# Three of four transposes per block move from TensorE to VectorE's 32x32 transpose (mLSTM block with a gated MLP)

## The reference

```python
xn = layernorm(x)
# mLSTM: 8 heads, 32 query/key and 64 value features each
q, k, v, o = xn @ Wq.T, xn @ Wk.T, xn @ Wv.T, xn @ Wog.T
i, f = soft_cap(xn @ Wig.T + big), soft_cap(xn @ Wfg.T + bfg)
h = mlstm_scan(q, k, v, i, f)                    # state carried over the tokens
att = (sigmoid(o) * multihead_norm(h, gamma)) @ Wout.T
# MLP, hidden size 2048
ffn = (silu(xn @ w_gate.T) * (xn @ w_up.T)) @ w_down.T
out = x + att + ffn
```

## Time and profile before

| | |
|---|---|
| Time, median of 3 runs | 3275.84 us (3273.61 to 3276.95) |
| The profiled execution's own time | 3273.61 us |
| Its span, first to last instruction | 3271.9 us |
| PE busy | 3101.0 us, 95% |
| DVE busy | 1876.5 us, 57% |
| ACT busy | 1116.8 us, 34% |
| POOL busy | 768.3 us, 23% |
| Granted TensorE clock, mean | 0.992 of full speed |

### The profile page before, as it was taken

How to read it: one execution, slowest core, us unless ns; L and a number is a source line. 1 busy time by engine, 2 the same in 40 slices (tenths; PEclk the granted TensorE clock), 3 DMA queues, 4 the chain that set the end, 5 groups by cost and what they waited for, 6 DMA issues and landing times.

```text
span 3271.9 us, 61574 instructions
## 1 busy us (share of the span) xinstructions
PE 3101.0 (95%) x22408; PEld 2229.5 (68%) x22408; DVE 1876.5 (57%) x4361; ACT 1116.8 (34%) x2142; POOL 768.3 (23%) x1126
## 2 busy tenths in 40 slices
PE   1499999999999999999999999999999999999999
PEld 0377777677776677776677776677776677776676
DVE  5565555565555565555665555655555655555654
ACT  3433333333333333333333333333333333333332
POOL 4322222222222222222222222222222222222122
PEclk9799999999999999999999999999999999999999
DMA  5000000000000000000000000000000000000000
GB/s 213 7 14 7 6 13 13 13 13 6 6 13 13 13 13 6 6 13 13 13 13 6 6 13 13 13 13 6 6 13 13 13 13 6 6 13 13 13 13 6
DMA packets 20333, 51.08 MB, mean 16 GB/s; under 512 B 1506, under 2 KB 1634, under 8 KB 18274
## 3 DMA queue, kind: packets, MB, share of 16 engines
q1 hardware_dynamic: 20322, 50.95, 4.2%
HBM read 34.16 MB, written 16.78 MB: 16 GB/s over the span
## 4 chain that ended last, share of the span: by engine, by line
issue 74%; POOL 21%; PE 2%; ACT 1%; POOLq 1%; DVE 1%; DVEq 0%; ACTq 0%
POOL arena L530 9%; POOL pair_r L520 4%; POOL small L549 3%; POOL arena L540 2%; POOL begun L537 1%; POOL small L430 1%; PE work L1006 0%; PE work L1008 0%; PE work L1007 0%; POOLq L529 0%; POOL parts_u L481 0%; PE acc L1006 0%; DVE parts_d L740 0%; PE acc L1008 0%; PE acc L1007 0%
## 5 line engine op out<-in xcount | busy, mean ns | idle before, releaser
L530 POOL TENSOR_TENSOR arena<-arena 128x256 f16<-128x256 f32 x512 | 348.1, 680 | 1769.9 <-ACT arena L644 1769.9
L879 DVE SCALAR_TENSOR_TENSOR arena<-arena,work 128x256 f32<-128x256 f32 x512 | 215.8, 422 | 634.4 <-ACT arena L640 628.0
L1006 PE MATMUL work<-xt,parts_g 128*128 128x256 f16 x2048 | 558.4, 273 | 0.0
L1007 PE MATMUL work<-xt,parts_g 128*128 128x256 f16 x2048 | 558.3, 273 | 0.0
L1006 PE MATMUL work<-xt,parts_u 128*128 128x256 f16 x2048 | 558.2, 273 | 0.0
L1007 PE MATMUL work<-xt,parts_u 128*128 128x256 f16 x2048 | 558.2, 273 | 0.0
L1008 PE MATMUL work<-xt,parts_u 128*128 128x256 f16 x2048 | 558.2, 273 | 0.0
L1008 PE MATMUL work<-xt,parts_g 128*128 128x256 f16 x2048 | 558.2, 273 | 0.0
L1006 PE MATMUL acc<-parts_d,arena 128*128 128x512 f16 x1024 | 388.8, 380 | 56.6 <-POOL arena L530 56.6
L640 ACT ACTIVATE arena<-work,unscale 128x256 f32<-128x256 f32 x512 | 240.9, 470 | 583.6 <-PE work L1008 581.0
L644 ACT ACTIVATE arena<-arena 128x256 f16<-128x256 f32 x512 | 213.8, 418 | 645.5 <-DVE arena L882 645.5
(11 more groups left out here) (214 smaller groups left out, 5503.9 us busy)
## 6 DMA issues: line engine op xcount, KB each, us to landing
arena<-x_dram SPq DMA_DIRECT2D x33, 512.0 KB, 3.3
out_dram<-arena SPq DMA_DIRECT2D x32, 512.0 KB, 2.8
parts_u<-w_g_dram SPq DMA_DIRECT2D x4, 1024.0 KB, 14.9
parts_d<-w_u_dram SPq DMA_DIRECT2D x4, 1024.0 KB, 22.8
arena<-w_d_dram SPq DMA_DIRECT2D x4, 1024.0 KB, 9.8
arena<-w_qk_dram SPq DMA_DIRECT2D x1, 1024.0 KB, 5.0
arena<-w_v_dram SPq DMA_DIRECT2D x1, 1024.0 KB, 7.0
arena<-w_o_dram SPq DMA_DIRECT2D x1, 1024.0 KB, 9.0
```

The lines of the kernel that those rows point to most:

```text
L530: g.tensor_tensor(hh[:, j % HB, 1, :], tt[:, j % 2, :], hh[:, j % HB, 0, :], ALU.subtract).then_inc(h_ready, 1)
L879: own.step(d.scalar_tensor_tensor(out=tt[:, j % 2, :], in0=tt[:, j % 2, :], scalar=1.0, in1=b[:, 0:BLOCK], op0=ALU.add, op1=ALU.mult))
L1006: t.matmul(dst, w[0], a[0], start=first, stop=False, skip_group_check=True)
L1007: t.matmul(dst, w[0], a[1], start=False, stop=False, skip_group_check=True)
```

## The change

Steps `xT0`, `xT1` and `hoT0` leave PE, and their three uses leave the bank list, which now has 33. In their place DVE transposes 32x32 squares: one call of `turn` takes 32 tokens of a chunk and issues four STREAM_TRANSPOSE instructions, each from 32 partitions (tokens) to 32 others (features), 128 float32 per partition. Four calls make a chunk, 16 instructions; three chunks make 48 per block. The calls are spread over `AFTER[7]` to `AFTER[14]`. `hoT1` stays on PE. `xn` now has room for one chunk only, so ACT's `xn1` waits for `turn03`; `xnt`, the transposed copy, holds two, and its second half also takes the transposed `hof` of chunk 0.

```diff
-         "ffn6", "st0", "ffn7", "ffn8", "st1", "ffn9", "ffn10", "st2", "ffn11", "hoT0", "ffn12", "st3", "o1",
-         "ffn13", "att0", "ffn14", "ffn15", "hoT1", "xT0", "xT1", "att1"])
+         "ffn6", "st0", "ffn7", "ffn8", "st1", "ffn9", "ffn10", "st2", "ffn11", "ffn12", "st3", "o1",
+         "ffn13", "att0", "ffn14", "ffn15", "hoT1", "att1"])
-AFTER[8] = ["es2", "pv1", "center0"]
-AFTER[9] = ["scale0", "xn1"]
-AFTER[10] = ["heads0", "es3", "pv2"]
-AFTER[11] = ["hoT0"]
-AFTER[12] = ["pv3", "o1", "center1"]
-AFTER[13] = ["att0", "scale1"]
-AFTER[14] = ["heads1"]
+AFTER[7] = ["turn00", "turn01"]
+AFTER[8] = ["es2", "pv1", "center0", "turn02"]
+AFTER[9] = ["scale0", "turn03", "xn1"]
+AFTER[10] = ["heads0", "es3", "pv2", "hoTurn0", "hoTurn1"]
+AFTER[11] = ["hoTurn2", "hoTurn3", "hoT0"]
+AFTER[12] = ["pv3", "o1", "center1", "turn10"]
+AFTER[13] = ["att0", "scale1", "turn11"]
+AFTER[14] = ["heads1", "turn12", "turn13"]
 AFTER[15] = ["hoT1", "xT0", "xT1"]
...
+                def turn(dst, src, q, turned):
+                    tokens = slice(q * 32, (q + 1) * 32)
+                    for r in range(P // 32):
+                        features = src[tokens, :].rearrange("t (k r f) -> t r k f", k=KC, f=32)[:, r, :, :]
+                        d.transpose(dst[r * 32:(r + 1) * 32, :, tokens], features).then_inc(turned, 1)
...
-                        elif step.startswith("hoT"):
+                        elif step == "hoT0":
+                            act.wait_ge(ho_turned, (i + 1) * TURNS)
+                            s.activation(ho[:, 0, :, :], xnt[:, 1, :, :], ACT.Copy).then_inc(ho_hi, 1)
+                        elif step == "hoT1":
...
                         elif step.startswith("xn"):
+                            act.wait_ge(xn_turned, START + i * NCH * TURNS + k * TURNS)
                             norm_x(i + 1, k)
                         elif step.startswith("xT"):
-                            wait_full(act, i, step)
-                            x_high(i + 1, k, bank(step)[:, :])
+                            act.wait_ge(xn_turned, START + i * NCH * TURNS + (k + 1) * TURNS)
+                            s.activation(xt[:, :, 0, k * P:(k + 1) * P], xnt[:, k, :, :], ACT.Copy).then_inc(xt_hi, 1)
...
+                elif step.startswith("hoTurn"):
+                            if k_ == 0:
+                                dve.wait_ge(ho_ready, START + i * NCH + 1)
+                            turn(xnt[:, 1, :, :], hof, k_, ho_turned)
```

More of the change, by code:

```diff
@@ L136 @@
 START = 1
+TURNS = 16
 DVE_OWN = 58
@@ L215, in mlstm_mlp_kernel @@
                  ("hof", 512), ("hoh", 512), ("kp", 512), ("tt", 512), ("hh", 768), ("res", 1024),
-                 ("wtok", NCH * 72), ("xn", NCH * D), ("qq", 1024), ("kk", 1024),
+                 ("wtok", NCH * 72), ("xn", D), ("xnt", NCH * KC * P), ("qq", 1024), ("kk", 1024),
                  ("state", NG * GW), ("wr", 256), ("tg", 256), ("uhl", 256), ("xin", 1024)]
@@ L236, in mlstm_mlp_kernel @@
         xin = at["xin"].rearrange("p (c d) -> p c d", c=NCH)
-        xn = at["xn"].rearrange("p (c d) -> p c d", c=NCH)
+        xn = at["xn"]
+        xnt = at["xnt"].rearrange("p (c k t) -> p c k t", c=NCH, k=KC)
         qs = at["qs"].rearrange("p (g t) -> p g t", g=NG)
@@ L306, in mlstm_mlp_kernel @@
         xn_ready = sem("xn_ready")
+        xn_turned = sem("xn_turned")
         xt_hi = sem("xt_hi")
+        ho_turned = sem("ho_turned")
+        ho_split = sem("ho_split")
         xt_ready = sem("xt_ready")
@@ L485, in _ @@
             for n, started in enumerate((*work_free, out_stored, res_done, exp_done, p_ready, num_ready, ho_ready,
-                                         state_ready)):
+                                         state_ready, xn_turned)):
                 g.memset(begun[0:1, n:n + 1], 0.0).then_inc(started, START)
@@ L588, in norm_x @@
                 act.wait_ge(factors_ready, i + 1)
-                s.activation(xn[:, c, :], xin[:, c, :], ACT.Identity, bias=shift[:, c:c + 1],
+                s.activation(xn, xin[:, c, :], ACT.Identity, bias=shift[:, c:c + 1],
                              scale=rstd[:, c:c + 1]).then_inc(xn_ready, 1)
@@ L752, in means, with x_low @@
                     d.bn_aggr(mean_var[:, c, :], bn6[:, c, :]).then_inc(stats_ready, 1)
-            def x_low(i, c, src, done):
+            def x_low(i, c, src):
                 dve.wait_ge(xt_hi, NCH * i + c + 1)
-                d.tensor_tensor(xt[:, :, 1, c * P:(c + 1) * P], src.rearrange("p (k t) -> p k t", k=KC),
-                                xt[:, :, 0, c * P:(c + 1) * P], ALU.subtract).then_inc(done, 1)
+                d.tensor_tensor(xt[:, :, 1, c * P:(c + 1) * P], src, xt[:, :, 0, c * P:(c + 1) * P],
+                                ALU.subtract).then_inc(xt_ready, 1)
             maxima(0)
@@ L790, in _ @@
             for c in range(NCH):
-                x_low(0, c, (e_bank, s_bank)[c][:, :], xt_ready)
+                x_low(0, c, (e_bank, s_bank)[c][:, :].rearrange("p (k t) -> p k t", k=KC))
             low_parts(1)
@@ L980, in _ @@
                                                    op1=ALU.mult).then_inc(ho_ready, 1)
-                        elif step.startswith("hoT"):
+                        elif step.startswith("hoTurn"):
+                            if k_ == 0:
+                                dve.wait_ge(ho_ready, START + i * NCH + 1)
+                            turn(xnt[:, 1, :, :], hof, k_, ho_turned)
+                        elif step == "hoT0":
+                            dve.wait_ge(ho_hi, i * NCH + 1)
+                            d.tensor_tensor(ho[:, 1, :, :], xnt[:, 1, :, :], ho[:, 0, :, :],
+                                            ALU.subtract).then_inc(ho_split, 1)
+                        elif step == "hoT1":
                             dve.wait_ge(ho_hi, i * NCH + k_ + 1)
@@ L984, in _ @@
                                             ho[:, 0, :, :], ALU.subtract).then_inc(free_of(step), 1)
+                        elif step.startswith("turn"):
+                            c = int(step[-2])
+                            dve.wait_ge(xn_ready, NCH * (i + 1) + c + 1)
+                            if (c, k_) == (1, 0):
+                                dve.wait_ge(ho_split, i + 1)
+                            turn(xnt[:, c, :, :], xn, k_, xn_turned)
                         elif step.startswith("xT"):
-                            wait_full(dve, i, step)
-                            x_low(i + 1, k_, bank(step)[:, :], free_of(step))
+                            x_low(i + 1, k_, xnt[:, k_, :, :])
                         elif step == "att0":
@@ L1029, in _ @@
                 for k in range(KC):
-                    tr = t.transpose((e_bank, s_bank)[c][:, k * P:(k + 1) * P], xn[:, c, k * P:(k + 1) * P],
+                    tr = t.transpose((e_bank, s_bank)[c][:, k * P:(k + 1) * P], xn[:, k * P:(k + 1) * P],
                                      ident[:, :])
                 tr.then_inc(first_xt, 1)
-            pe.wait_ge(xt_ready, NCH)
             with pe.Fori(0, NB) as i:
@@ L1049, in project @@
                 def project(c):
-                    wait_drained(pe, i, f"hoT{c}")
+                    if c == 0:
+                        pe.wait_ge(ho_split, i + 1)
+                    else:
+                        wait_drained(pe, i, "hoT1")
                     for n in range(KC):
@@ L1055, in project @@
                     mm_.then_inc(work_full, 1)
+                pe.wait_ge(xt_ready, NCH * (i + 1))
                 wait_bank(pe, i, "gates")
-                pe.wait_ge(work_free[bank_no("xT1")], START + i * uses_of(bank_no("xT1")))
                 for k in range(KC):
```

## The result

The changed kernel takes 3403.76 us, median of 4 runs (3403.16 to 3404.17), against 3275.86 before: a ratio of 1.0396, 95% interval 1.0383 to 1.0408. It is slower, as forecast, but by 128 us where 58 were forecast, and it lies above the top of the stated range, 3390.

The account below looks back on a forecast made before the run. PE's own stream was taken to bound the kernel. Per block -1.31 + 1.75 + 1.37 = +1.81 us, +58 us over 32 blocks, gave 3334 us, 1.8% slower; the 8-in-10 range was 3250 to 3390.

Parts of the forecast that it names:

- stall A: PE waits ahead of slice 13 for DVE's late pair of slice 12: 1.75 us per block.
- rival 4: PE's clock falls because of the new gaps; held that nothing speaks for it, with no chance of its own.
- What bounds the kernel: PE's own stream sets the time, 96.66 of 98.41 us per block; the old wait ahead of down(0) stays.
- What leaves PE: Transposes of xT0, xT1 and hoT0 leave PE: 1.31 us less per block, 41.9 us over 32 blocks.
- Price of a transpose: Each DVE transpose takes 0.31 us from start to start, without overlap; bounds 0.21 and 0.45 us.
- the prediction's own formula: With a transpose at t, stall A is 1.75 + 24 (t - 0.31) and stall B 1.37 + 8 (t - 0.31) per block.
- upper t, 0.38: Highest transpose price in the main forecast, t 0.27 to 0.38 us with both stalls, 3290 to 3390, chance 0.60.
- Stall B: PE waits ahead of down(15) for POOL's low part, late through turn12 and turn13: 1.37 us per block.
- The bank of slice 11 ... just holds.: Slice 11's bank is free at 3143.4, and o1 wants it no sooner than 3143.75, so no wait there.

Follow-up runs that it names:

- e5: Changed kernel with all 48 DVE transposes moved into DVE's idle times, xn in two tiles, transposed hof in kp: 3235.3 us, ratio 0.9874 to before.
- e7: Changed kernel with turn12 and turn13 moved from AFTER[14] to AFTER[15], ahead of and behind hoT1: 3367.09 us, ratio 1.0271 to before.
- e3: Changed kernel with ACT's copy and DVE's low part of hoT0 moved behind slice 12's tanh and pair: 3340.05 us, ratio 1.0196 to before.
- e4: Changed kernel with room for both chunks of normed x, so xn1 doesn't wait for turn03: 3342.73 us, ratio 1.0203 to before.

## Why the prediction was right in kind and wrong in size

Two of its steps failed: the size of stall A, 1.75 us where 2.93 came, and rival 4, which put the clock at nothing where it cost 25 us. Either alone would have left the time inside the range. By its own steps:

- **What bounds the kernel.** Right. What PE does not issue is gained if nobody keeps it waiting (e5), and the wait ahead of `down(0)` was unchanged, 1.75 us.
- **What leaves PE, 1.31 us.** Right: e5 gives it whole.
- **Price of a transpose, 0.31 us.** Nearly right. The group of the changed kernel in the view by line, and a call of `turn` in DVE's timeline:

```profile
L839 DVE STREAM_TRANSPOSE arena<-arena 32x128 f32<-32x128 f32 x1536 | 464.2, 302 | 45.0
```

```profile
3156.55 1.31 DVE L839 STREAM_TRANSPOSE arena<-arena 32x128 f32<-32x128 f32 x4
```

  Each takes 0.302 us, and four take 1.31 from first start to last end, so starts are 0.336 apart ((1.31 - 0.30) / 3); eight in 2.65 give the same. They don't overlap, which agrees with the Trainium skill's rule on instructions whose start quarter changes ("VectorE: DVE Perf Modes", section "Two Vector instructions with no wait between them"). That the quarter is the reason only the copies show; no run has transposes in a row that all write the same one. POOL did not hold them: `turn03` ran beside POOL's power and took its 1.31 us. The 0.026 us that the price was short of are not small here: by the prediction's own formula they make 32 x 0.026, 0.83 us per block, and a forecast of 3361 instead of 3334. By the same formula its upper t, 0.38, gives 3405, so the range's top of 3390 was too low for the prices that it was meant to cover.
- **Stall B, 1.37.** Right in place; the idle time is 1.38 and the delay 1.55 us, which e7 takes away. With t at 0.336 the formula gives 1.58.
- **Stall A, 1.75.** Right in its chain, too small: 2.93 us. This is the term that was mis-sized most. The rows of the changed kernel, DVE first, then POOL and ACT (the changed kernel's block lies 23.38 us later than the one of before, 3093.27 less 3069.89):

```profile
3159.11 0.42 DVE L897 SCALAR_TENSOR_TENSOR arena<-arena,work 128x256 f32<-128x256 f32 x1 [1.24 <-ACT arena L646]
...
3160.91 0.95 DVE L995 SCALAR_TENSOR_TENSOR arena<-arena 128x512 f32<-128x512 f32 x1
3162.62 0.75 DVE L939 SCALAR_TENSOR_TENSOR arena<-s_bank,unscale,arena 128x512 f32<-128x512 f32 x1 [0.75 <-POOL arena L546]
...
3164.15 2.62 DVE L839 STREAM_TRANSPOSE arena<-arena 32x128 f32<-32x128 f32 x8
...
3167.71 2.65 DVE L839 STREAM_TRANSPOSE arena<-arena 32x128 f32<-32x128 f32 x8
...
3172.11 0.42 DVE L900 SCALAR_TENSOR_TENSOR arena<-arena,work 128x256 f32<-128x256 f32 x1
```

```profile
3160.51 0.81 POOL L536 TENSOR_TENSOR arena<-arena 128x256 f16<-128x256 f32 x1 [2.26 <-ACT arena L650]
3161.28 0.63 POOL L543 TENSOR_TENSOR begun<-half_pow 1x1 f32<-1x1 f32 x1
3161.87 0.63 POOL L546 TENSOR_SCALAR_AFFINE_SELECT arena<-arena 128x512 f32<-128x512 f32 x1
```

```profile
3157.90 0.82 ACT L595 ACTIVATE arena<-arena,small 128x512 f32<-128x512 f32 x1 [2.56 <-DVE arena L839]
...
3170.39 0.63 ACT L680 ACTIVATE arena<-arena 128x512 f16<-128x512 f32 x1 [2.26 <-DVE arena L839]
```

  Every link is there. Slice 10's pair starts at 3159.11, in the old clock 3135.73, forecast 3135.6. The mask of `es3` ends at 3139.12, forecast 3138.4: POOL's one-element instruction ahead of it took 0.63 instead of 0.18 us, beside DVE's line 995 with two inputs in the same memory, and the low part of slice 10 in front of it 0.81 instead of 0.67; that put 0.6 us into the chain. The sixteen `hoTurn` transposes took 0.3 more. PE started 0.13 us after DVE's last instruction ended (3172.53 to 3172.66), which I counted in B and forgot in A. With the 0.13 at slice 10 that makes up the 1.18 us.
- **"The bank of slice 11 ... just holds."** Wrong: `o1` waited 0.45 us. The pair of slice 11 ended at 3167.68, in the old clock 3144.30 and not 3143.4. That wait is within the 2.93.
- **Rival 4, the clock.** Wrong, and the larger lesson. I dismissed it because a gap of 1.75 us left the clock at 1.00. The gap that came was 2.16 us in one piece, and 25 us went with it.

The account in all: forecast +58 us; 38 us from A (1.18 for each of 32 blocks), 6 from B (0.18), 3 from slice 13's first matmuls (0.10) and 25 from the clock give 130; the two spans differ by 133, with the last 3 us mostly outside the equal blocks (the first gates come 1.3 us later), and the medians by 128. The forecast's structure held: both stalls, their chains and their causes were as named, and e3, e4, e7 and e5 each moved what the walk said they would. The range was too narrow on the slow side because it had no room for the clock, and because nearly all errors in a walk of ten links lay on one side.

## What to carry to other kernels

Moving work from a full engine to one that is half idle pays only where the other is idle at that moment: read its idle stretches one by one, and put the work ahead of the instruction that would have waited anyway; the same 48 instructions cost 128 us in one placing and gave 42 in the other. Work taken out of the bounding engine may also have been what covered a chain behind it, as the transposes ahead of `down(15)` did. And when a walk forecasts a wait of the matmul engine as long as the longest that the trace shows at full clock, or longer, the clock is one more term of the sum.

## What was not expected of the hardware

- PE's clock fell to half for 3.4 us behind a wait of 2.16 us in 15 of 32 blocks, and in 21 with the same wait in e7. It cost 25 us here and some 60 us at a wait of 2.41 us, and did not fall behind waits of 1.58 or 1.75 us.
- An instruction of POOL on one element takes 0.185 us in 96 of 128 executions. In the other 32 it runs beside DVE's line 995, an instruction with two inputs from the same memory, and takes 0.632 to 0.636 us. DVE's transposes did not suffer from POOL in this way: 448 that ran beside it took 0.303 us in the mean, the other 1088 took 0.302.
